# Decoder layer on one core: the router's columns are streamed with the base projection, and the last three tiles are reordered

## The reference, cut to what matters

```python
h   = x + mamba2(rmsnorm(x), ...)               # one chunk of 128 tokens per sequence
y   = h + (silu(n2 @ gate.T) * (n2 @ up.T)) @ down.T      # n2 = rmsnorm(h); 1792 wide
x1  = layernorm(y)
x2  = layernorm(x1 + softmax(x1 @ ctx.T) @ ctx)
lg  = x2 @ gate_w.T + expert_bias               # 4 experts; the winner is one-hot(argmax)
z   = (x2 @ lora_A.T) * winner                  # 4 experts x rank 8 = 32 columns
out = layernorm(x2 + x2 @ W_up.T + z @ lora_B.T)
```

## Time and profile before

| | |
|---|---|
| median of 3 runs | 409.71 us (409.71, 409.72, 407.6) |
| profiled execution, its own time | 409.69 us |
| its span, first to last instruction | 407.9 us |
| mean granted TensorE clock | 0.997 |
| PE busy | 390.9 us (96%) |
| DVE busy | 291.6 us (71%) |
| ACT busy | 193.3 us (47%) |
| POOL busy | 140.2 us (34%) |
| chain that ended last, by engine | PE 69%, DVE 20%, ACT 7% |

### The profile page before, as it was taken

One profiled execution on the slowest core, in us unless ns is written; L12 is line 12 of the kernel. 1 busy time (PEld: TensorE's weight loads), 2 busy tenths in 40 slices (PEclk: granted clock), 3 DMA queues, 4 the chain that ended last, 5 costly groups with the idle time before them and its releaser, 6 DMA issues.

```text
span 407.9 us, 5321 instructions
## 1 busy us (share of the span) xinstructions
PE 390.9 (96%) x1892; PEld 312.6 (77%) x1896; DVE 291.6 (71%) x518; ACT 193.3 (47%) x389; POOL 140.2 (34%) x128
## 2 busy tenths in 40 slices
PE   7999999998979989999999999999999999999984
PEld 3778887665669978888888888887788788787753
DVE  3489981257885778989797979695467657675676
ACT  5678676946664574351524243863313234142131
POOL 5505525834434555556472737830000000000000
PEclk9999999999999999999999999999999999999998
DMA  8801110110001014111213111441110120110002
GB/s 272 276 23 52 53 51 0 52 53 0 1 2 47 7 58 149 53 51 51 61 45 102 49 57 53 152 157 51 53 52 27 52 77 26 51 51 27 27 2 78
DMA packets 11659, 25.52 MB, mean 63 GB/s; under 512 B 1681, under 2 KB 1809, under 8 KB 11634
## 3 DMA queue, kind: packets, MB, share of 16 engines
q1 hardware_dynamic: 10482, 23.10, 17.3%
q10 hardware_dynamic: 1152, 2.10, 1.4%
HBM read 23.10 MB, written 2.10 MB: 62 GB/s over the span
## 4 chain that ended last, share of the span: by engine, by line
PE 69%; DVE 20%; ACT 7%; issue 2%; POOL 1%; ACTq 0%; DVEq 0%
PE bank L609 19%; PE bank L611 19%; PE bank L610 19%; DVE big L1466 5%; PE bank L731 2%; PE bank L871 2%; PE bank L882 1%; DVE sets_f L1533 1%; DVE big L1501 1%; PE bank L893 1%; DVE sets L1521 1%; PE bank L620 1%; DVE big L1454 1%; DVE tmp L1710 1%; PE bank L853 1%
## 5 line engine op out<-in xcount | busy, mean ns | idle before, releaser
L609 PE MATMUL bank<-sets,station 128*128 128x512 f32 (+1 forms) x424 | 164.3, 388 | 1.8 <-DVE station L1581 1.2
L610 PE MATMUL bank<-sets,station 128*128 128x512 f32 (+1 forms) x424 | 158.7, 374 | 0.0
L611 PE MATMUL bank<-sets,station 128*128 128x512 f32 (+1 forms) x424 | 158.7, 374 | 0.0
L609 PEld LDWEIGHTS bank<-sets,station 128*128 128x128 f32 x424 | 80.1, 189 | 19.5 <-issue 3.5
L610 PEld LDWEIGHTS bank<-sets,station 128*128 128x128 f32 x424 | 80.0, 189 | 15.2 <-issue 2.1
L611 PEld LDWEIGHTS bank<-sets,station 128*128 128x128 f32 x424 | 79.9, 188 | 14.3
L567 POOL TENSOR_TENSOR big<-tmp,side_f 128x512 f32<-128x512 f32 x17 | 26.4, 1568 | 24.0 <-DVE side_f L1597 24.0
L1309 ACT ACTIVATE small<-small 128x1 f32<-128x1 f32 x24 | 7.1, 294 | 48.2 <-DVE small L1712 48.2
L1466 DVE SCALAR_TENSOR_TENSOR big<-bank,cw,big 128x508 f32<-128x508 f32 (+2 forms) x36 | 26.2, 738 | 2.3 <-ACT big L1062 1.4
L1597 DVE TENSOR_TENSOR side_f<-side_f,bank 128x512 f32<-128x512 f32 x36 | 24.6, 684 | 4.1 <-PE bank L611 3.8
L472 POOL TENSOR_TENSOR station<-raw,station 128x1024 fp32r<-128x1024 f32 x7 | 16.8, 2397 | 26.3 <-ACT station L992 26.3
(11 more groups left out here) (189 smaller groups left out, 675.4 us busy)
## 6 DMA issues: line engine op xcount, KB each, us to landing
raw<-wstream SPq DMA_DIRECT2D x31, 512.0 KB, 3.4
rows<-x SPq DMA_DIRECT2D x8, 256.0 KB, 4.6
big<-ctxT SPq DMA_DIRECT2D x8, 256.0 KB, 2.7
big<-ctx SPq DMA_DIRECT2D x8, 256.0 KB, 3.0
out<-tmp ACTq DMA_DIRECT2D x8, 256.0 KB, 2.0
big<-ln_w SPq DMA_DIRECT2D x1, 256.0 KB, 5.4
big<-lora_b SPq DMA_DIRECT2D x3, 64.0 KB, 5.0
ga<-gate_lora SPq DMA_DIRECT2D x1, 72.0 KB, 5.3
```

The lines of the kernel that those rows point to most:

```text
L609: pe.matmul(ps, a_hi, b_lo, start=first, stop=False)
L610: pe.matmul(ps, a_hi, b_hi, start=False, stop=False)
L611: return pe.matmul(ps, a_lo, b_hi, start=False, stop=last)
```

## The change

The parts are these. (1) The 36 routing columns are split into FP32R parts too, by two GpSimd operations once, and stand behind the 512 columns of the base weights (`baseS`, 548 columns for each part and chunk). (2) `base(t, side, ...)` streams them in two sides: side 1 is base columns 256 to 511 with the 36 routing columns (292 columns) into the upper bank of a pair, side 0 is base columns 0 to 255 into the lower. Side 1 signals route_ps. `route` of TensorE is gone. (3) ACT writes x2's high part straight from PSUM, and DVE takes the low part from PSUM: the cast and the buffer x2T are gone. (4) z is transposed into bank 2 (or 1), `lora` is two matmuls of 256 columns, `add_ffn` reads the two banks of the pair. (5) In the ending, all three lists are reordered, DVE's `route` is cut into `choose` (three operations) and `routed` (the rest), and the four unread matmuls are left out. (6) Two small buffers (`xb`, `cs3`) move within SBUF to make room, and banks 0, 1 and 6, 7 are allocated as pairs. The diff, cut to its core:

```diff
@@ -65,7 +65,9 @@
 SETS_AT = RAW_AT + 2 * CH
 STATION_AT = SETS_AT + N_SET * 2 * CH
 SIDE_AT = STATION_AT + 7 * CH
-ARENA = SIDE_AT + 4 * CH
+N_ROUTE = E + E * RANK
+BASE_N = D + N_ROUTE
+ARENA = SIDE_AT + 2 * DC * BASE_N
 
 SEQ = tuple((g, n) for g in range(G0, LAST_GATE) for n in range(7)) + (
     (LAST_GATE, P1), (LAST_GATE, P6), (LAST_GATE, P5), (LAST_GATE, P7), (LAST_UP, P1), (LAST_GATE, P3),
...
         LN1_BANK = 7
 
-        bank = [es.enter_context(nc.psum_tensor(f"bank{i}", [P, D], F32)) for i in range(8)]
+        first_pair = es.enter_context(nc.psum_tensor("bank_first", [P, 2, D], F32))
+        middle = [es.enter_context(nc.psum_tensor(f"bank{i}", [P, D], F32)) for i in range(2, 6)]
+        last_pair = es.enter_context(nc.psum_tensor("bank_last", [P, 2, D], F32))
+        bank = [first_pair[:, i, :] for i in range(2)] + middle + [last_pair[:, i, :] for i in range(2)]
+        pair_of = {0: first_pair, 6: last_pair}
 
...
                     up_product(g, 2, st_c21, u2u3[1])
             pool.wait_ge(st_c21, N_GROUP - G0)
             pool.memset(zm, 0.0).then_inc(zm_clear, 1)
+            pool.wait_ge(up11_ok, NM // 2 - 1)
+            pool.wait_ge(up_ok, 3 * (NM // 2 - 1) - 1)
+            pool.tensor_copy(baseS[:, 0, :, D:BASE_N], ga[:, :, :]).then_inc(ga_hi, 1)
+            pool.wait_ge(ga_hi, 1)
+            pool.tensor_tensor(baseS[:, 1, :, D:BASE_N], ga[:, :, :], baseS[:, 0, :, D:BASE_N].bitcast(F32),
+                               ALU.subtract).then_inc(ga_lo, 1)
...
-            def route(t, bk=7, halves=False):
-                pe.wait_ge(x2_ok, t + 2 if halves else t + 1)
-                for c in range(DC):
-                    mm = pe.matmul(bank[bk][:, 0:E + E * RANK], x2T[:, bass.ts(c, P)], ga[:, c, :],
-                                   start=(c == 0), stop=(c == DC - 1))
-                mm.then_inc(route_ps, 1)
-
-            def base(t, first_use=False, bk=6, halves=False):
-                pe.wait_ge(x2_lo, t + 1)
-                if first_use:
-                    pe.wait_ge(bw_lo, 2)
-                elif bk == 6:
-                    pe.wait_ge(ln_u[2], t)
-                for c in range(DC):
-
-                    if halves and c == 2:
+            def base(t, side, chunks=range(DC), first_use=False, pair=6, halves=False, free=None):
+
+                if side == 1 and 0 in chunks:
+                    pe.wait_ge(x2_lo, t + 1)
+                    if first_use:
+                        pe.wait_ge(bw_lo, 2)
+                        pe.wait_ge(ga_lo, 1)
+                    elif pair == 6:
+                        pe.wait_ge(ln_u[2], t if free is None else free)
+                cols = slice(0, D // 2) if side == 0 else slice(D // 2, BASE_N)
+                ps = bank[pair + side][:, 0:cols.stop - cols.start]
+                for c in chunks:
+
+                    if halves and side == 1 and c == 2:
                         pe.wait_ge(x2_lo, t + 2)
-                    q, k = bass.ts(c, P), bass.ts(c, D)
-                    three_pass(pe, bank[bk][:, :], x2S[:, 0, q], x2S[:, 1, q], sideS[:, 0, k], sideS[:, 1, k],
-                               c == 0, False)
-
-            def turn_z(t):
+                    q = bass.ts(c, P)
+                    mm = three_pass(pe, ps, x2S[:, 0, q], x2S[:, 1, q], baseS[:, 0, c, cols], baseS[:, 1, c, cols],
+                                    c == 0, side == 1 and c == DC - 1)
+                if side == 1 and DC - 1 in chunks:
+                    mm.then_inc(route_ps, 1)
+
+            def turn_z(t, bk=2):
                 pe.wait_ge(zm_ok, t + 1)
-                pe.transpose(bank[7][:, P:2 * P], zm, ident[:, :]).then_inc(zmT_ps, 1)
-
-            def lora(t, bk=6):
+                pe.transpose(bank[bk][:, 0:P], zm, ident[:, :]).then_inc(zmT_ps, 1)
+
+            def lora(t, pair=6):
                 pe.wait_ge(zmT_ok, t + 1)
-                pe.matmul(bank[bk][:, :], zmT[:, :], lbS[:, :], start=False, stop=True).then_inc(ffn_ps, 1)
+                for i in range(2):
...
+                    mm = pe.matmul(bank[pair + i][:, 0:D // 2], zmT[:, :], lbS[:, bass.ts(i, D // 2)],
+                                   start=False, stop=True, skip_group_check=(i == 1))
+                mm.then_inc(ffn_ps, 1)
...
                 if f:
-                    route(t - 2)
-                    base(t - 2, first_f)
+                    base(t - 2, 1, first_use=first_f)
+                    base(t - 2, 0)
...
             down(last, 1, 4, False, END_SEGS)
-            route(last - 2)
-            base(last - 2)
+            base(last - 2, 1)
+            base(last - 2, 0)
             turn_x2(last - 1, 0)
             turn_halves(last, u1, ln_out[0], (2, 0), q_ps)
-            turn_z(last - 2)
             attend(last, 1, halves=True)
+            turn_z(last - 2, bk=1)
             lora(last - 2)
             turn_ex(last)
-            route(last - 1)
+            base(last - 1, 1, range(1), pair=0)
             mix(last)
-            base(last - 1)
+            base(last - 1, 1, range(1, DC), pair=0)
+            base(last - 1, 0, pair=0)
             turn_halves(last, u2[:, 1, :], ln_out[1], (3, 5), x2_ps)
-            keep_warm(4, 2, wd(0, 0)[:, 0:P], wd(0, 0))
             turn_z(last - 1)
-            route(last, bk=1, halves=True)
-            lora(last - 1)
-            base(last, bk=0, halves=True)
+            base(last, 1, range(2), halves=True, free=last - 1)
+            lora(last - 1, pair=0)
+            base(last, 1, range(2, DC), halves=True)
+            base(last, 0)
             turn_z(last)
-            lora(last, bk=0)
+            lora(last)
 
...
                 act.wait_ge(raw_in[raw_slot(n)], landed(n))
-                act.activation(sideS[:, 0, bass.ts(i, CH)], raw[:, raw_slot(n), :], ACT.Copy).then_inc(bw_hi, 1)
+                act.activation(baseS[:, 0, bass.ts(i, 2), 0:D], in_two(raw[:, raw_slot(n), :]), ACT.Copy).then_inc(bw_hi, 1)
...
                 act.wait_ge(x2_ps, t + 1)
-                act.activation(x2T, bank[3][:, :], ACT.Copy).then_inc(x2_ok, 1)
+                act.activation(x2S[:, 0, :], bank[3][:, :], ACT.Copy).then_inc(x2_hi, 1)
 
             def copy_halves(t, dst, ready, banks, done):
...
             rstd(0, last)
+            copy_halves(last, qT, q_ps, (2, 0), q_ok)
             copy_x2(last - 1)
-            copy_halves(last, qT, q_ps, (2, 0), q_ok)
-            copy_z(last - 2)
+            copy_z(last - 2, bk=1)
             exp_scores(last)
+            rstd(2, last - 2)
             rstd(1, last)
-            copy_halves(last, x2T, x2_ps, (3, 5), x2_ok)
+            copy_halves(last, x2S[:, 0, :], x2_ps, (3, 5), x2_hi)
             copy_z(last - 1)
-            rstd(2, last - 2)
             store(last - 2)
             copy_z(last)
             rstd(2, last - 1)
...
 
-            def route(t, bk=7):
+            def choose(t, bk=7):
 
                 v.wait_ge(route_ps, t + 1)
-                v.tensor_tensor(lg[:, 0, :], bank[bk][:, 0:E], eb[:, :], ALU.add).then_inc(lg_step, 1)
+                v.tensor_tensor(lg[:, 0, :], bank[bk][:, D // 2:D // 2 + E], eb[:, :], ALU.add).then_inc(lg_step, 1)
                 v.wait_ge(lg_step, 5 * t + 1)
...
                 v.tensor_reduce(gm[:, 0:1], lg[:, 0, :], AX.X, ALU.max).then_inc(lg_step, 1)
                 v.wait_ge(lg_step, 5 * t + 2)
                 v.scalar_tensor_tensor(out=lg[:, 1, :], in0=lg[:, 0, :], scalar=gm[:, 0:1], in1=codes[:, :],
                                        op0=ALU.is_equal, op1=ALU.mult).then_inc(lg_step, 1)
+
+            def routed(t, bk=7):
+
                 v.wait_ge(lg_step, 5 * t + 3)
                 v.tensor_reduce(gm[:, 1:2], lg[:, 1, :], AX.X, ALU.max).then_inc(lg_step, 1)
                 v.wait_ge(lg_step, 5 * t + 4)
...
 
+            def route(t, bk=7):
+                choose(t, bk)
+                routed(t, bk)
+
             def add_mlp(t, par):
 
                 v.wait_ge(down_ps, t + 1)
                 v.tensor_tensor(u1, bank[par][:, :], rows[:, bass.ds(t, 1), :].rearrange("p a n -> p (a n)"),
                                 ALU.add).then_inc(ln_u[0], 1)
 
-            def add_ffn(t, par, u=u3, bk=6, stored_tiles=None):
+            def add_ffn(t, par, u=u3, pair=6, stored_tiles=None):
 
                 v.wait_ge(ffn_ps, t + 1)
                 if stored_tiles is not None:
                     v.wait_ge(stored, 16 * stored_tiles)
-                v.tensor_tensor(u, bank[bk][:, :], u2[:, par, :], ALU.add).then_inc(ln_u[2], 1)
-
-            def split_x2(t):
-                v.wait_ge(x2_ok, t + 1)
-                v.tensor_copy(x2S[:, 0, :], x2T).then_inc(x2_hi, 1)
+                v.tensor_tensor(in_two(u), pair_of[pair][:, :, 0:D // 2], in_two(u2[:, par, :]), ALU.add) \
+                    .then_inc(ln_u[2], 1)
+
+            def low_x2(t):
                 v.wait_ge(x2_hi, t + 1)
-                v.tensor_tensor(x2S[:, 1, :], x2T, x2S[:, 0, :].bitcast(F32), ALU.subtract).then_inc(x2_lo, 1)
-
```

(31 more changed lines are left out.)

25 lines of the change are left out of this document (14 added, 11 removed).

## The result

The changed kernel ran at 404.32 us (median of 6 runs, 403.63 to 404.95), the kernel before beside it at 409.31 (6 runs, 407.6 to 409.79). The ratio is 0.9889 with a 95% interval of 0.9867 to 0.9911. The forecast was 405.6 us and 4.1 us less than before; 5.0 us less was measured.

A forecast was written before the change was run, and what follows sets the result against it. TensorE's own work was taken to bound the loop, and one chain of DVE, ACT, PE, DVE the ending. 409.69 - 2.6 (five tiles of 0.52) - 1.5 (ending) = 405.6 us, range 403.4 to 407.7.

The forecast's parts named there:

- A 292-column distance: In the loop's base stream, start to start of 292-column matmuls, interpolated between 0.120 and 0.231 us: 0.1356 us.
- Saving of a tile: In each loop tile, routing and base take 3.15 us instead of 3.67, saving 0.52 us.
- The slack of 0.18 us ahead of side 1: In a loop tile, x2's low part ends at 345.87, TensorE reaches side 1 at 346.05; some 0.05 goes to the semaphore.
- Row maximum of tile 7: In the ending, tile 7's row maximum comes 1.25 us earlier, at 388.6 on the old clock.
- The 0.08 us: In a tile's base stream, an extra paid once where plain float32 gives way to FP32R.
- The comparison with the back-to-back figures: For the base stream, the skill's lone-matmul figures make new base cost 0.21 us more, the trace rows 0.22.
- Cost nothing: Bank pair, added wait for GpSimd's two operations and moved buffers cost nothing; if not covered, about 1 us once.
- A: Rival: the loop gains, the ending doesn't, 407.1 us; chance 0.09.
- B: Rival: x2's low part comes late in every tile and replaces what was saved, 408.2 us; chance 0.05.
- C: Rival: without the four unread matmuls TensorE's clock falls to 1.2 GHz in the ending, 408.1 us; chance 0.05.
- D: Rival: weight loads stop overlapping, each of a tile's 24 matmuls costs 0.19 us, 413.6 us in all; chance 0.05.
- two separate gains: Loop and ending each gain: 2.6 us over five tiles, 1.5 us in the ending, added together.

The follow-up runs named there:

- cast_kept: The changed kernel with x2's old path: ACT copies to x2T, VectorE casts the high part and subtracts from x2T; 407.07 us, ratio 0.9961.
- split_512_36: The changed kernel with the 548 columns streamed as 36 and 512 instead of 292 and 256, lora one of 512; 412.46 us, ratio 1.0102.

## Why the prediction was right

The forecast direction and mechanism held, and the time lay in the range. Step by step, with the ending counted from the transposes of x1 of tile 6:

- A 292-column distance: forecast 0.1356 us, measured 0.1355. 256 columns: 0.120, measured 0.1175.
- Saving of a tile: forecast 0.52, measured 0.59 (2.96 over five). The stream gave 0.53; the other 0.06 is the passage from the scores, 0.81 us from their start to side 1 where 0.89 stood before. cast_kept and split_512_36 show that a tile saves 0.59 us only with both the wide sides and the missing cast.
- The slack of 0.18 us ahead of side 1, "less some 0.05": TensorE didn't wait, but by less than I had reckoned. The subtraction ended 0.13 us ahead of side 1, and cast_kept shows that TensorE needs 0.13 or 0.05 us of that to start. Between nothing and 0.07 us was left. A cast on this path cost 0.45 us a tile in four of five tails.
- Row maximum of tile 7: forecast 1.25 us earlier, measured 1.35. Attention's addition 1.55, measured 1.62. End of tile 6's routing 2.2, measured 2.27. Start of tile 7's routing 0.96, measured 1.13. z turned 1.58, measured 1.76. Last normalisation 1.5, measured 1.69.
- The 0.08 us, "paid once where plain float32 gives way to FP32R": the size was right, the reason wasn't. In split_512_36 the first 512-column distance behind 36-column matmuls of FP32R is 0.33 us (347.31 to 347.64) where the next is 0.22, with no plain float32 near.
- The comparison with the back-to-back figures: the rows' difference between the new and the old base is 12 x (0.1356 + 0.120 - 0.231) = 0.30 us with the 0.08 left out of both, not 0.22, and measured it is 0.26. So the trace doesn't agree with the difference of 0.21 either. The forecast doesn't use it.
- "Cost nothing": the step that failed. GpSimd's two operations on the routing columns cost 0.5 us, because they ran beside VectorE's split of the down weights, for which TensorE waits. I had named what hides them on GpSimd and had not looked at what VectorE does at that time.
- The rivals: A and B did not occur. C did not occur in the changed kernel's traced execution, and the fillers bought nothing; in split_512_36 the clock did fall in the ending. D did not occur, but the distance does stop shrinking somewhere below 256 columns (0.111 us at 36).
- My picture of two separate gains was too simple. In the ending the merged stream needs the new order; alone it gives nothing.

The sum without the start is 4.16 us against the 4.1 forecast, and so close by luck: +0.36 in the loop and +0.19 in the ending make up for the -0.49 ahead of them. The rest of the measured 5.0 us in the medians lies within what the starts and the clock of single executions do: runs of one kernel differ by up to 2.4 us.

## What to carry to other kernels

A narrow product that shares its stationary operand with a wide one costs almost only its columns when it rides on it (36 columns more took 0.018 us a matmul), provided that each matmul stays wide enough; given a bank of its own at 36 columns, it took 0.111 us a matmul. Before a short operation is called free, look at every engine that works at the same time, not only at its own queue. Where a merge makes a result later and an order decides who waits for it, change both together and test each alone: the traces cut at fixed instructions tell tenths that medians can't.
